# First FFN weight: seven groups loaded at the end of the last stage, a semaphore for each, multiplied in that order

## What is computed

```python
logits = jnp.einsum('bsd,ed->bse', x, gate_w) + gate_b
probs = jax.nn.softmax(logits, axis=1)
vals, idx = jax.lax.top_k(probs.transpose(0, 2, 1), K)          # K = 8
gathered = jnp.take_along_axis(x, flat_idx[:, :, None], axis=1)
pooled = jnp.einsum('bked,bke->bed', gathered, topv)
h = jax.nn.gelu(jnp.einsum('ebd,edh->ebh', [pooled, 1], weight1), approximate=False)
out = jnp.einsum('eho,ebh->ebo', weight2, [h, 1])               # 64 experts, 128 -> 512 -> 128
outputs = zeros.at[flat_idx].add(out * topv)                    # scattered back, then x + outputs
```

## Time and profile before

| | us |
|---|---|
| median of 3 runs | 2889.62 (2883.52 to 2896.89) |
| the profiled execution | 2896.19 |
| its span, first to last instruction | 2894.4 |
| stage 1, about | 0 to 1150 |
| stage 2, about | 1150 to 1850 |
| stage 3 | 1880 to 2786 |
| tail | 2786 to 2894.4 |

### The profile page before, as it was taken

One profiled execution on the slowest core, in us unless ns is written; L12 is line 12 of the kernel. 1 busy time (PEld: TensorE's weight loads), 2 busy tenths in 40 slices (PEclk: granted clock), 3 DMA queues, 4 the chain that ended last, 5 costly groups with the idle time before them and its releaser, 6 DMA issues.

```text
span 2894.4 us, 65116 instructions
## 1 busy us (share of the span) xinstructions
PE 2609.9 (90%) x15070; PEld 2141.5 (74%) x15070; DVE 2415.4 (83%) x4683; ACT 2253.1 (78%) x4278; POOL 1828.9 (63%) x1911
## 2 busy tenths in 40 slices
PE   6999999999999998999999999489899898898935
PEld 5888888888888887988898898366666666666623
DVE  6777777777777776999999999889999888989862
ACT  5888888888888887788888888478888888888840
POOL 8888888888888886000000000099999999999941
PEclk9999999999999999999999999799999999999977
DMA  5777777777777776899999999599999999999946
GB/s 185 264 271 272 268 265 273 270 264 272 272 267 266 274 270 252 315 334 332 339 324 339 333 338 332 185 354 364 366 365 368 362 356 359 364 359 359 363 137 213
DMA packets 281418, 873.06 MB, mean 302 GB/s; under 512 B 29479, under 2 KB 81858, under 8 KB 281378
## 3 DMA queue, kind: packets, MB, share of 16 engines
q1 hardware_dynamic: 272322, 855.31, 80.4%
q10 hardware_dynamic: 8704, 16.78, 2.0%
q0 software_dynamic: 352, 0.53, 0.2%
HBM read 492.97 MB, written 379.52 MB: 301 GB/s over the span
## 4 chain that ended last, share of the span: by engine, by line
PE 43%; DMA 21%; DVE 9%; issue 9%; POOL 8%; ACT 5%; SPq 3%; DVEq 1%; POOLq 0%; ACTq 0%
PE banks L1285 34%; DMA arena<-left_d 12%; DMA work<-gate_d 7%; PE banks L1274 4%; POOL arena L689 3%; POOL arena L695 2%; DVE bn L1102 2%; ACT arena L825 2%; ACT work L895 2%; PE banks L1320 1%; DVE arena L1093 1%; PE banks L1371 1%; POOL rs L712 1%; DMA work<-in_x_dram 1%; DVE arena L1082 1%
## 5 line engine op out<-in xcount | busy, mean ns | idle before, releaser
L1285 PE MATMUL banks<-x_parts,w_parts 128*128 128x512 f32 x4320 | 1068.0, 399 | 0.0
L1285 PEld LDWEIGHTS banks<-x_parts,w_parts 128*128 128x128 f32 x4320 | 791.7, 189 | 161.7
L1320 PE MATMUL banks<-left_parts,right_parts 128*128 128x384 f32 x3456 | 629.1, 340 | 60.3 <-ACT arena L826 49.5
L1320 PEld LDWEIGHTS banks<-left_parts,right_parts 128*128 128x128 f32 x3456 | 603.7, 190 | 85.8 <-issue 81.7
L973 DVE SCALAR_TENSOR_TENSOR arena<-banks,cols,arena 128x512 f32<-128x512 f32 x576 | 407.0, 748 | 246.9 <-ACT arena L791 245.1
L684 POOL COPY rcol<-late 128x8 f32 (+1 forms) x144 | 28.4, 197 | 715.1 <-ACT late L841 715.1
L895 ACT ACTIVATE work<-arena,rs 128x128 f32<-128x128 f32 x1152 | 352.5, 389 | 128.1 <-POOL rs L712 128.1
L1353 PE MATMUL banks<-wo_sb,arena 128*128 128x128 f32 x2304 | 396.2, 301 | 9.1 <-DVE arena L1093 8.6
L689 POOL TENSOR_TENSOR arena<-arena,work 128x512 f32<-128x512 f32 x288 | 359.7, 1270 | 61.9 <-DVE arena L1082 61.2
L1353 PEld LDWEIGHTS banks<-wo_sb,arena 128*128 128x128 f32 x2304 | 359.8, 192 | 50.1 <-issue 21.1
L651 POOL TENSOR_TENSOR x_parts<-xn,x_parts 128x512 fp32r<-128x512 f32 x288 | 372.0, 1292 | 6.6 <-ACT x_parts L779 6.6
(11 more groups left out here) (177 smaller groups left out, 4165.9 us busy)
## 6 DMA issues: line engine op xcount, KB each, us to landing
arena<-in_x_dram SPq DMA_DIRECT2D x144, 512.0 KB, 3.4
left_d<-arena SPq DMA_DIRECT2D x144, 512.0 KB, 2.6
right_d<-arena SPq DMA_DIRECT2D x144, 512.0 KB, 3.4
gate_d<-arena SPq DMA_DIRECT2D x144, 512.0 KB, 4.2
arena<-right_d SPq DMA_DIRECT2D x128, 576.0 KB, 5.7
arena<-left_d SPq DMA_DIRECT2D x128, 576.0 KB, 6.7
mixed_d<-arena SPq DMA_DIRECT2D x128, 576.0 KB, 4.4
work<-mixed_d SPq DMA_DIRECT2D x144, 512.0 KB, 4.8
```

Of the source, the lines that this page charges most:

```text
L1285: last = nc.tensor.matmul(ps[2 + k][:, :], w_parts[:, wq, k], x_parts[:, xq, b, c], start=((wq, xq) == TERMS[0]), stop=((wq, xq) == TERMS[ ...
L1320: last = nc.tensor.matmul(ps[NT * b + t][:, 0:GRID], lr_parts[RIGHT][:, rq, b, k, t * P:(t + 1) * P], lr_parts[LEFT][:, lq, b, k], start=( ...
```

## The change

The seven groups 0 to 6 of the first weight are no longer loaded between pieces of stage 3's loop. ACT issues them in one series of 14 loads of 1 MB (one j with all four bands each), at the head of its drain iteration 72, when SP has issued the loads of the last step. Each group has a semaphore of its own. TensorE multiplies in the order 0 to 7 and waits for each group. SP issues `load_w2(n)` for n >= 1 after n groups and not n + 1, and GpSimd's memset over group 7 waits for all eight. Group 7 is loaded behind the stage, as before.

```diff
-        s_w1 = sem("s_w1")
+        s_w1 = [sem(f"s_w1{n}") for n in range(WLOADS)]
@@ SP, tail
             for n in range(1, WLOADS):
-                sp.wait_ge(s_h1, n + 1)
+                sp.wait_ge(s_h1, n)
                 load_w2(n)
@@ GpSimd, tail
-            pool.wait_ge(s_h1, 1)
+            pool.wait_ge(s_h1, WLOADS)
             nc.gpsimd.memset(win2_words[0], 0.0).then_inc(s_clear, 1)
@@ ACT
             def load_w1(n):
-                j, first = n // 2, BANDS // 2 * (n % 2)
-                some = slice(first, first + BANDS // 2)
-                act.dma_start(w1_sb[:, j, some], w1_view[j, :, some]).then_inc(s_w1, 16)
+                for j in range(2 * n, 2 * n + 2):
+                    act.dma_start(w1_sb[:, j], w1_view[j]).then_inc(s_w1[n], 16)
@@ ACT, stage3
                 for b in range(2):
+                    if isinstance(i, int) and 2 * i + b == STEPS:
+                        for n in range(WLOADS - 1):
+                            load_w1(n)
                     if in_range(i, b, 0, STEPS):
                         scale_rest(i, b)
@@
-            cuts = [lambda n=n: load_w1(n) for n in range(4 * (WLOADS - 1))]
-            pairs(act, STEPS, stage3, drain=2, cuts=cuts)
+            pairs(act, STEPS, stage3, drain=2)
@@
-            for n in range(4 * (WLOADS - 1), 4 * WLOADS):
-                load_w1(n)
+            load_w1(WLOADS - 1)
@@ TensorE, tail
-            pe.wait_ge(s_w1, 16 * 2 * SIDE)
-
-            order = (WLOADS - 1,) + tuple(range(WLOADS - 1))
-            for n in order:
+            for n in range(WLOADS):
+                pe.wait_ge(s_w1[n], 32)
                 for j in (2 * n, 2 * n + 1):
                     for g in range(BANDS):
                         last = nc.tensor.matmul(ps[2][BAND * g:BAND * (g + 1), :], win1[:, g, BAND * j:BAND * (j + 1)],
-                                                w1_sb[:, j, g], start=(j == 2 * order[0]), stop=(j == 2 * order[-1] + 1))
+                                                w1_sb[:, j, g], start=(j == 0), stop=(j == SIDE - 1))
                 last.then_inc(s_h1, 1)
```

## The result

The changed kernel takes 2903.0 us (median, 2899.6 to 2908.8) where the kernel before takes 2889.9: a ratio of 1.0039, 95% interval 1.0023 to 1.0055. Timed a second time beside other kernels the ratio was 1.0048 (1.0029 to 1.0066). So it is slower by 7 to 19 us, about 13. The forecast was 2.7 us faster, 2887. The time lies inside the range given; the sign doesn't.

A forecast was written before the change was run, and what follows sets the result against it. GpSimd was taken to set the loop's rhythm, which late transfers break, and a chain of waits the tail. -31 + 30.0 - 1.7 = -2.7 from 2889.62 gave 2887 us; own range 2877 to 2899, eight in ten 2868 to 2904.

The forecast's parts named there:

- Part 1: Stage 3's loop: taking out 28 loads of 0.5 MB on ACT's queue saves 31 us (21 to 34).
- Part 2: Drain iteration 72: 14 loads hold ACT, exponential of step 140 comes 28.6 us later, stage's end 30.0 later (24 to 34).
- the term for TensorE's half clock: End of stage 3: after idling, TensorE's three serial groups run at half speed, 8.0 us for 5.96, +2.1.
- The rival of free issue: Drain iteration 72: 14 loads issue at 0.49 us each, small copies lose 4 us; sum -25.4, 2864 us; chance 0.14.
- Parts 3 and 4: Tail: small copies meet no backlog and TensorE waits for no group, 0 (0 to 3); new group order, -1.7 us (-1.7 to 0).
- The loop that doesn't quicken: Stage 3's loop: its remaining transfers keep steps near 6.10, saving 9.5 us and not 31; 2908 us; chance 0.09.

The follow-up runs named there:

- order_only: The kernel before with only group order 0 to 7, SP's waits one group earlier and the window memset behind all eight groups; one execution, 2891.8 us.
- before_again: The kernel before, unedited, timed against itself and profiled once more; 2890.5 us beside 2885.1, ratio 1.0007.
- sp_series: Changed kernel with the table load ahead of the loop, all 16 first-weight loads issued by SP, the tail's small copies by ACT; 2875.2 us, 0.9953 against the kernel before.

## Why the prediction was wrong, point by point

Averages of the profiles: loop 879.7 (three profiles, order_only's loop being the same) to 859.8 (two), -19.9; tail 122.8 to 150.0 (two each, as order_only's tail is changed), +27.2; together +7.3. That is the sum to be set against -2.7.

- **Part 1, the step that failed.** "That ACT has one loop in place of 29 costs or gives nothing: ACT isn't what the others wait for there." Splitting the loop did more than spread the loads. Measured: +6.7 us; with this term alone the sum of -2.7 would have been +4.0, and the sign right. Nor was it so that the others don't wait for ACT there: GpSimd's `residual_rest` does, once the table load stands ahead of `scale_rest`. The evidence was in the trace of the kernel before. The three steps of 6.02, which the prediction took as a bound for a step without loads, were the steps of the two iterations with a table load; and grouped by line, the table load stood there with a count of two. 6.02 was set aside for the later cycle and not asked for its cause, yet it is within 0.01 of what the whole loop then did (860.0/143 = 6.01).
- **Part 1, the size.** Without the table load the loads' removal gives 879.7 - 853.1 = 26.6 us, 0.95 for each load, and not 31. Part of that is the one profile it was read from: its loop is 2.1 us above the mean of three. The rest is a step of 5.97 (853.1/143) and not 5.95. The 26.6 lie within the bounds of 21 to 34; the 19.9 that the loop gave in all lie just below them. No run keeps the 29 pieces without their loads, so what the cutting itself cost, if anything, is inside the 26.6.
- **Part 2, the standstill.** Right, in mechanism and size: 28.4 us against 28.6; the series 30.9 us against 31.5. That ACT's queue behaves as SP's, which no row showed, is measured now. What is left of the stage behind that exponential was to be 1.4 us longer (-0.7 + 2.1) and is 0.7 shorter, since the term for TensorE's half clock was counted from the wrong base. +2.1 was forecast, and the three groups took 6.11 us against 5.96. Their rows in TensorE's timeline of the changed kernel:

```profile
2789.25 2.36 PE L1371 MATMUL banks<-yt,gate_t 128*64 128x512 f32 x4 [29.86 <-ACT yt L885]
2791.54 1.97 PE L1363 MATMUL banks<-ident,work 128*128 128x128 f32 x8
2793.48 1.78 PE L1371 MATMUL banks<-yt,gate_t 128*64 128x512 f32 x4
```

These answer to the last three of the earlier trace rows and came after 30 us of idling, at a granted clock of 0.50 from 2788 to 2792 (1.2 GHz, the lower level) and 0.64 in the two microseconds behind. Each is within 0.13 us of its row before, because that profile had the lower level there too. In its windows of 2 us (columns as in the earlier trace rows) the clock falls from 1.00 while the first of the three groups runs:

```profile
2778.00:2780.00 2.00, 2.00 (x6) 0.42 (x4) 0.13 (x1) 0.48 (x2) 0.00 (x0) 0.51 0.00 0
2780.00:2782.00 2.00, 2.00 (x9) 1.38 (x8) 1.34 (x3) 0.97 (x2) 0.19 (x1) 0.64 0.01 4
```

In before_again, the same program, the clock was 1.00 over these groups (it had been down for the two groups ahead of them), and they took 4.02 us:

```profile
2772.84 1.46 PE L1371 MATMUL banks<-yt,gate_t 128*64 128x512 f32 x4 [0.96 <-ACT yt L886]
2774.23 1.09 PE L1363 MATMUL banks<-ident,work 128*128 128x128 f32 x8
2775.70 1.47 PE L1371 MATMUL banks<-yt,gate_t 128*64 128x512 f32 x4 [0.39 <-ACT yt L886]
```

So the lower level costs these three groups 2.1 us, as forecast, but the 5.96 us from which the forecast counted had most of it in them. From the exponential of step 140 to the last one it is 12.3 us in the profile on record and 10.7 in before_again: part of the scatter of the tail before.

- **The Trainium skill's rule** ("DMA: Bandwidth & Descriptors", "Issuing engines are not separate DMA queues": the sequencer's time to start a transfer is usually small beside it) fits three loads of 1 MB, at 0.43 to 0.59 us. For the series it doesn't: the issues took 30.9 us, and 14.7 MB at 390 GB/s are 37.7 us. The rival of free issue falls. Its 4 us for small copies in a backlog were too few as well: sp_series shows 11.4 for two of them, and its bound, 1.74 more for each, was passed by both (3.4 and 8.0).
- **Parts 3 and 4.** Right: no small copy met the backlog, TensorE waited for no group, and the order gave 1.2 to 1.5 of 1.7 us.
- **The loop that doesn't quicken** was the rival nearest to what came, with another cause: the loop quickened by 19.9 us, two thirds of the forecast.

Put together: -31 + 4.4 (size) + 6.7 (table load) + 27.2 (the tail, where 30.0 - 1.7 = 28.3 was foreseen) = +7.3. The timed runs say 13 (7 to 19). What makes the rest isn't settled: the profiles are one execution each, and the start of stage 3 alone scatters by 14 us among them.

## What to carry to other kernels

A long series of transfers holds the engine that issues it for about as long as the data take, less what fits in the queue (3 MB here). So ask what stands behind the series on that engine, and give it to one with nothing urgent behind it. When the split of a loop changes, list what its body holds on each engine, function-table loads included, and look at the first iterations of the old trace: steps there that differ by a tenth of a microsecond have a cause. And small transfers on the critical chain want an empty queue; the place for bulk is where the DMA engines idle and nobody waits.

## What the runs showed of the hardware beyond that

- An ACT table load takes 1283 ns, each of 68. The Trainium skill ("ScalarE: Activation LUTs", "What ACT_TABLE_LOAD costs") gives the same 1283 ns and adds a drain of some 1380 ns; here the next instruction starts 1.29 us after the load does, so no such addition is seen. Nor is it at the first of the 68, the one that changes the table and doesn't repeat it (load at 1913.81, next instruction at 1915.10). Of its 1.28 us for two steps, 0.64 a step, the loop lost 0.095 a step where no transfer was late; the rest lay in ACT's waits.
- A small copy suffers from a backlog far more than its size tells: the token numbers (four copies of 1 KB) went from 1.85 to 9.8 us, the 4 KB of pack_hi from 1.74 to 5.1, the gather from some 5.5 to 11.4.
- Issues of ACT run ahead of its arithmetic also at iteration 72: the first of the series went out 0.6 us after the start of a normalise with five of its instructions and two copies still ahead of it.
